# Four transposes of each even attention step move from the middle of the query projection to the gap behind the sums of squares

## The chip, the cores and the metric

The kernel runs on one core of one Trainium2 chip. The metric is the device time of the whole program in microseconds (us), the median of several runs. In the names of the profile PE is TensorE's matrix multiplications, PEld its weight loads, DVE is VectorE, ACT is ScalarE, POOL is GpSimd and SP is the engine that issues most DMAs.

## What is computed

A gated cross-attention layer and then a mixture of experts, on 32 sequences of 64 tokens (2048 rows of 512 numbers), all in float32. The attention has 32 query heads of 128, grouped by four on 8 key-value heads, and normalises each query and key by its root mean square.

```
x = x + tanh(g_xattn[0]) * attention(layernorm(x), ctx)
x = x + tanh(g_ffn[0]) * moe(layernorm(x))
attention:
  q = rmsnorm(h @ Wq.T) ; k = rmsnorm(ctx @ Wk.T) ; v = ctx @ Wv.T
  probs = softmax(q @ k.T / sqrt(128) + mask)
  return (probs @ v) @ Wo.T
moe:
  shared = silu(h @ Gs) * (h @ Us) @ Ds
  top 2 of 16 experts by softmax(h @ gate), weights normalised
  return weighted sum of the experts' outputs + shared
```

## The kernel before, in words

The program has three stages: keys, values and transposed inputs (to 215 us of the profiled run), the attention loop (215 to 1145 us), and the experts with the shared layer (the rest). The change lies in the attention loop alone.

**Number format.** Products that need float32 accuracy are split: an operand x is kept as a rounded high part and the low rest, and `split_product` (lines 549 to 551) adds three products, high by low, low by high and high by high. So ScalarE writes a high part (`pth`, `ah`, `w0h`) and VectorE then subtracts it to get the low part (`ptl`, `al`, `w0l`).

**The loop.** It has 64 steps, numbered i from 0. A step belongs to one pair of sequence blocks and one pair of heads; even and odd steps differ in where their results lie. Each engine has its own hand-written order of the work of a step, and semaphores tie them together. Three steps' work is in flight at a time, so that in step i TensorE issues, in this order (`step`, line 681 on):

- the query projection of step i+1 for head 0 (12 matmuls of 128x512, here "Q") and half of that of head 1 (6 matmuls);
- four transposes (`transpose_probs`, line 642) of the probabilities `pb` that the softmax of step i has made. In an even step they fill the PSUM bank `PS[6]`, in an odd one halves of `PS[2]` and `PS[3]`. They wait for `p_ready`, which VectorE's last two multiplications of the softmax raise (line 1324);
- the other 6 matmuls of the query projection;
- the products of probabilities and values of step i-1 (`probs_v`, line 657), the scores of step i+1 (line 615), and the sums of squares of its queries (`q_sums`, line 623), which the softmax of step i+1 starts from;
- the output products (`outputs`), 12 matmuls into `PS[7]` and 12 into `PS[6]`. The second dozen waits until VectorE has taken the transposes out of `PS[6]` (`pT_evac`).

ScalarE (`act_step`) copies and squares the queries, casts the transposes to `pth` (`probs_hi`, line 1038 in even steps), casts the value products to `ah` (`a_hi_tile`, line 1046; the second pair waits for the first dozen of output products), and takes the exponentials (line 1022). In an even step the cast of line 1038 also waits for the value products of the same step, which still read the `pth` of before.

VectorE (`dve_step`) starts a step with the low part of the transposes (`probs_lo`, line 1333 in even steps) and of the first value products (`a_rest`, line 1290). Then comes `softmax`: it takes the sums of squares out of PSUM (line 1297, `sst`), adds a constant (`qv`, line 1299), and while GpSimd takes the inverse root (line 464) it does what `while_root` holds: it adds the first dozen of output products to the sums `acc` (line 1284) and splits the second pair of value products. Then it scales the scores (line 1306), masks them (1309), takes their maximum (1312) and difference (1315), adds the other dozen of output products, and finishes with sum, reciprocal and two multiplications (1319, 1321, 1324).

The first step (`first=True`) has its transposes behind the sums of squares already and no output products. The last even step, 62 (`last=True` on TensorE), has an order of its own on all three engines. In steps 58 to 61 VectorE has the first parts of the second layer norm to do besides (`residual`, lines 1345 and 1348, 1.4 us a row tile).

Of the kernel before, what the change touches and what calls it, by code (L numbers as in the profile page):

```python
# [63 lines left out]
def build(nc, x, ctxT, wk, wv, w_att, w_shd, mask, g_x, g_f, q_w, k_w, gate, w_gu, w_dn, out):  # L64
# [11 lines left out]
    with ExitStack() as ctx:  # L76
# [129 lines left out]
        with ExitStack() as a:  # L206
# [33 lines left out]
        pT_done, pT_evac, pv_done, a_hi, a_lo, o_done, acc_done = (  # L240
            sem("pT_done"), sem("pT_evac"), sem("pv_done"), sem("a_hi"), sem("a_lo"), sem("o_done"),
            sem("acc_done"))
# [311 lines left out]
        def _(pe):  # L554
# [133 lines left out]
            def step(d, odd, pair_q, w_q, w_before, w_o, q_ready=None, o_ready=None, first=False,  # L688
                     last=False):


                i = 2 * d + odd
                if q_ready is not None:
                    pe.wait_ge(w_lo, q_ready)
                pe.wait_ge(q_sq, 2 * i + 1)
                q_head(0, 1 - odd, pair_q, w_q).then_inc(q_done, 1)
                if last:
                    pe.wait_ge(ss_turned, i + 1)
                    transpose_h2(0, 2)
                    pe.wait_ge(s_scaled, i + 1)  # L700
                    transpose_h2(1, 3)
                pe.wait_ge(q_sq, 2 * i + 2)
                q_head(1, 1 - odd, pair_q, w_q, (0, 1))
                if not first:
                    if not odd:
                        pe.wait_ge(acc_done, 2 * i)
                    transpose_probs(i, odd)
                q_head(1, 1 - odd, pair_q, w_q, (2, 3)).then_inc(q_done, 1)
                if first:
                    pe.wait_ge(s_scaled, 1)  # L710
                    pe.wait_ge(ss_turned, 1)
                else:
                    probs_v(i - 1, 1 - odd)
                if last:
                    pe.wait_ge(h2T_lo, 2)
                scores(d + odd, 1 - odd)
                q_sums(i + 1)
                if last:
                    transpose_h2(2, 0)
                    transpose_h2(3, 1)  # L720
                if first:
                    transpose_probs(i, odd)
                else:
                    outputs(i - 1, w_before, w_o, o_ready)

            pe.wait_ge(w_lo, 4)
# [228 lines left out]
        def _(act):  # L955
# [59 lines left out]
            def squares(h, j):  # L1015
                act.wait_ge(ss_done, j + 1)
                act.activation(sq[:, h].rearrange("p b s -> p (b s)"), PS[h][:], ACT.Square).then_inc(q_sq, 1)
# [22 lines left out]
            def a_hi_tile(i, bp):  # L1040
                if bp == 1:
                    act.wait_ge(o_done, 2 * i + 1)
                    act.wait_ge(a_lo, 4 * i + 6)
                for b2 in range(2):
                    act.wait_ge(pv_done, 2 * i + 3 + b2)
                    act.copy(ah[:, bp, :, b2, :], pv_view(bp, b2)).then_inc(a_hi, 1)  # L1046
# [6 lines left out]
            def act_step(d, odd, w, sl, first=False):  # L1053
                i = 2 * d + odd
                act.wait_ge(s_done, i + 1)
                q_out(0, i + 1)
                squares(0, i + 1)
                if odd:
                    probs_hi(i, 1)
                q_out(1, i + 1)  # L1060
                squares(1, i + 1)
                if not odd:
                    probs_hi(i, 0)
                if not first:
                    a_hi_tile(i - 1, 0)
                    a_hi_tile(i - 1, 1)
                split_slice(i, w, sl)
                exps(i + 1)
# [142 lines left out]
        def _(dve):  # L1211
# [114 lines left out]
            def probs_lo(i, odd):  # L1326
                if odd:
                    for q in range(2):
                        dve.wait_ge(pT_hi, 2 * i + 1 + q)
                        dve.tensor_tensor(pt_odd(1, q), pT_odd(q), pt_odd(0, q), ALU.subtract).then_inc(pT_evac, 1)  # L1330
                else:
                    dve.wait_ge(pT_hi, 2 * i + 2)
                    dve.tensor_tensor(pt_even(1), pT_even(), pt_even(0), ALU.subtract).then_inc(pT_evac, 2)
# [16 lines left out]
            def dve_step(d, odd, w, sl, tile_before, tile, complete=(None, None), first=False):  # L1350

                i = 2 * d + odd
                probs_lo(i, odd)
                if complete[0] is not None:
                    residual(complete[0], 1)
                if not first:
                    a_rest(i - 1, 0)
                if complete[1] is not None:
                    residual(complete[1], 0)

                def while_root():
                    if not first:
                        add_out(2 * i - 1, 1, tile_before)
                        a_rest(i - 1, 1)

                def while_exp():
                    if not first:
                        add_out(2 * i, 0, tile)

                softmax(i + 1, while_root, while_exp)  # L1370
                slice_lo(i, w, sl)
# [370 lines left out]
```

## Time and profile before

| | |
|---|---|
| median of 3 runs | 1465.6 us (1465.59 to 1466.02) |
| the profiled execution, its own time | 1465.77 us |
| its span, first to last instruction | 1464.0 us |
| PE busy | 1419.2 us (97%) |
| PEld busy | 1128.1 us (77%) |
| DVE busy | 847.3 us (58%) |
| ACT busy | 501.0 us (34%) |
| POOL busy | 317.9 us (22%) |
| mean granted clock of TensorE | 0.991 of full speed |

The table reads as follows: the profile is of one execution, so every duration is compared with 1465.77 us, of which 1464.0 us is the span. TensorE is busy nearly always, and the other engines have room on average. "Busy" of PE counts overlapping pipelined matmuls once, so a busy PE can still issue more slowly than it might; the distance from one start to the next shows that.

### The profile page before, as it was taken

To read this page: it belongs to the slowest core of one execution; us is meant where nothing else is said; L and a number is where in the kernel's file an instruction comes from. 1 tells how busy PE (TensorE), PEld (TensorE's weight loads), DVE (VectorE), ACT (ScalarE), POOL (GpSimd) and SP (SyncE) were. 2 spreads that over 40 slices of the span, in tenths; PEclk is the share of its full clock that TensorE was granted. 3 is DMA by queue.
4 is the path that set the end of the run, shared out by engine and by line. 5 is a ranking of instruction groups with operands and counts; after the bars stand their busy time and mean duration, and the time that the engine had idled before them with its cause. 6 is when DMAs were issued, how large, how long until landed. Compare 5 with 4: busy or idle time off the path is not lost.

```text
span 1464.0 us, 27092 instructions
## 1 busy us (share of the span) xinstructions
PE 1419.2 (97%) x9085; PEld 1128.1 (77%) x9086; DVE 847.3 (58%) x1816; ACT 501.0 (34%) x1097; POOL 317.9 (22%) x330
## 2 busy tenths in 40 slices
PE   6999997999999999999999999999999999999995
PEld 5888876787777877778787777877777888777773
DVE  5444446565666656666565666656687653344375
ACT  4333343333333333333333333333334421222220
POOL 1222223212122121211212121121212101232462
PEclk9999999999999999999999999999999999999997
DMA  6544440111111111111101111111122343655565
GB/s 225 164 122 136 122 118 30 47 30 40 37 40 40 30 47 37 34 36 40 41 29 49 37 33 39 38 40 33 59 71 81 126 170 138 230 164 170 153 195 171
DMA packets 91097, 125.95 MB, mean 86 GB/s; under 512 B 7376, under 2 KB 56528, under 8 KB 90512
## 3 DMA queue, kind: packets, MB, share of 16 engines
q1 hardware_dynamic: 84704, 104.16, 22.5%
q0 software_dynamic: 6320, 20.71, 5.1%
q8 instruction: 58, 0.95, 0.3%
q14 instruction: 15, 0.12, 0.0%
HBM read 87.36 MB, written 37.49 MB: 85 GB/s over the span
## 4 chain that ended last, share of the span: by engine, by line
PE 91%; issue 3%; DVE 2%; DMA 2%; POOL 1%; ACT 1%; SPq 0%; POOLq 0%; DVEq 0%; ACTq 0%
PE ps L549 23%; PE ps L551 22%; PE ps L550 22%; PE ps L879 5%; PE ps L615 4%; PE ps L657 4%; PE ps L895 3%; PE ps L623 2%; PE ps L642 2%; PE ps L874 1%; PE ps L596 1%; DMA acc<-in_wv 1%; DMA wgu<-in_w_gu 1%; DVE acc L1660 1%; PE ps L793 1%
## 5 line engine op out<-in xcount | busy, mean ns | idle before, releaser
L1046 ACT CAST ah<-ps 128x256 fp32r<-128x256 f32 x256 | 83.4, 382 | 238.5 <-PE ps L551 234.6
L470 POOL CAST vth<-vt 128x256 fp32r<-128x256 f32 x64 | 25.7, 402 | 637.6 <-PE ps L657 637.6
L1284 DVE TENSOR_TENSOR acc<-ps,acc 128x512 f32 (+1 forms) x129 | 88.6, 687 | 129.9 <-PE ps L551 129.9
L549 PE MATMUL ps<-hT,w0h 128*128 128x512 f32 (+1 forms) x384 | 153.9, 401 | 0.9 <-DVE w0l L1232 0.9
L551 PE MATMUL ps<-hT,w0h 128*128 128x512 f32 (+1 forms) x384 | 150.6, 392 | 0.0
L550 PE MATMUL ps<-hT,w0l 128*128 128x512 f32 (+1 forms) x384 | 150.0, 391 | 0.0
L464 POOL TENSOR_TENSOR qr<-qv,mhalf 128x8 f32<-128x8 f32 x64 | 105.6, 1649 | 90.0 <-DVE qv L1299 90.0
L1290 DVE TENSOR_TENSOR al<-ps,ah 128x256 fp32r<-128x256 f32 x256 | 95.7, 416 | 50.6 <-ACT ah L1046 50.6
L1013 ACT COPY qs<-ps 128x512 f32<-128x512 f32 x128 | 75.2, 587 | 134.9 <-PE ps L551 131.4
L1022 ACT ACTIVATE pb<-pb 128x256 f32<-128x256 f32 x128 | 48.2, 418 | 175.3 <-DVE pb L1315 175.3
L549 PE MATMUL ps<-w1l,ah 128*128 128x512 f32 x260 | 105.3, 405 | 1.0 <-DVE al L1290 1.0
L549 PE MATMUL ps<-w0l,ah 128*128 128x512 f32 x256 | 103.8, 406 | 0.0
L549 PE MATMUL ps<-hT,w1h 128*128 128x512 f32 (+1 forms) x256 | 102.7, 401 | 0.0
L550 PE MATMUL ps<-w1h,al 128*128 128x512 f32 x260 | 102.1, 393 | 0.0
L551 PE MATMUL ps<-w1h,ah 128*128 128x512 f32 x260 | 101.3, 390 | 0.0
L550 PE MATMUL ps<-w0h,al 128*128 128x512 f32 x256 | 100.7, 393 | 0.0
L551 PE MATMUL ps<-hT,w1h 128*128 128x512 f32 (+1 forms) x256 | 100.2, 392 | 0.0
L551 PE MATMUL ps<-w0h,ah 128*128 128x512 f32 x256 | 99.7, 390 | 0.0
L550 PE MATMUL ps<-hT,w1l 128*128 128x512 f32 (+1 forms) x256 | 99.7, 390 | 0.0
L879 PE MATMUL ps<-wgu,xgT 128*128 x376 | 94.8, 382 | 0.3 <-issue 0.2
L551 PEld LDWEIGHTS ps<-hT,w0h 128*128 128x128 f32 x384 | 72.3, 188 | 15.6
L549 PEld LDWEIGHTS ps<-hT,w0h 128*128 128x128 f32 x384 | 72.3, 188 | 15.4 <-DVE w0l L1232 1.1
(223 smaller groups left out, 3033.8 us busy)
## 6 DMA issues: line engine op xcount, KB each, us to landing
wraw<-in_w_att SPq DMA_DIRECT2D x64, 256.0 KB, 2.6
ybuf<-ye SPq DMA_DIRECT2D x47, 256.0 KB, 2.0
vbuf<-vo SPq DMA_DIRECT2D x16, 512.0 KB, 3.3
kbuf<-ko SPq DMA_DIRECT2D x16, 512.0 KB, 3.8
kt<-kbuf SPq DMA_DIRECT2D x32, 256.0 KB, 2.9
vt<-vbuf SPq DMA_DIRECT2D x64, 128.0 KB, 2.0
wgu<-in_w_gu SPq DMA_DIRECT2D x4, 2048.0 KB, 9.3
craw<-in_ctxT SPq DMA_DIRECT2D x9, 512.0 KB, 4.9
```

What stands on the lines that cost most here:

```text
L464: pool.tensor_tensor(qr[:], qv[:], mhalf[:, 0:8], ALU.pow).then_inc(q_rt, 1)
L549: pe.matmul(dst, l_hi, r_lo, start=first, stop=False)
L550: pe.matmul(dst, l_lo, r_hi, start=False, stop=False)
L551: return pe.matmul(dst, l_hi, r_hi, start=False, stop=last)
L615: mm = pe.matmul(PS[3][h * S:(h + 1) * S, b * S:(b + 1) * S], qs[:, h, b], kt[:, b, :], start=True, stop=True)
L657: mm = pe.matmul(PS[4 + b2][:, bp * 256:(bp + 1) * 256], vhl[v_part][rows, bp, :], pt[p_part][rows, 2 * part + bp, :], start=(z == 0), sto ...
L879: mm = pe.matmul(PS[2 + q][:, 0:2 * EI], xgT[q][:, k, :], wgu[:, bass.ds(e, 1), k * 2 * EI:(k + 1) * 2 * EI].rearrange("p a n -> p (a n)") ...
L1013: act.copy(qs[:, h].rearrange("p b s -> p (b s)"), PS[h][:]).then_inc(q_copy, 1)
L1022: act.activation(pb[:, CB * hp:CB * hp + CB, :], pb[:, CB * hp:CB * hp + CB, :], ACT.Exp).then_inc(s_exp, 1)
L1046: act.copy(ah[:, bp, :, b2, :], pv_view(bp, b2)).then_inc(a_hi, 1)
L1284: dve.tensor_tensor(dst, PS[6 + bp][:], dst, ALU.add).then_inc(acc_done, 1)
L1290: dve.tensor_tensor(al[:, bp, :, b2, :], pv_view(bp, b2), ah[:, bp, :, b2, :], ALU.subtract).then_inc(a_lo, 1)
```

## The change

In even steps other than the last, TensorE's four transposes move from between the two halves of head 1's query projection to behind the sums of squares, ahead of the output products, and the query projection runs through its 24 matmuls. Thirty steps (2, 4, ... 60) change so; step 0 has that place already. On ScalarE the cast of the transposes in even steps goes behind the first pair of casts `ah`. On VectorE the low part of the transposes in even steps goes from the head of the step into `while_root`, behind `sst` and `qv` and ahead of the addition of line 1284; this holds for step 0 too. Odd steps keep their order. No instruction is added or taken away, and no semaphore changes its count.

```
# TensorE, step()
-                if not first:
-                    if not odd:
-                        pe.wait_ge(acc_done, 2 * i)
+                if last:
+                    pe.wait_ge(acc_done, 2 * i)
+                if odd or last:
                     transpose_probs(i, odd)
                 q_head(1, 1 - odd, pair_q, w_q, (2, 3)).then_inc(q_done, 1)
...
-                if first:
+                if not odd and not last:
+                    if not first:
+                        pe.wait_ge(acc_done, 2 * i)
                     transpose_probs(i, odd)
-                else:
+                if not first:
                     outputs(i - 1, w_before, w_o, o_ready)
# ScalarE, act_step()
+                if not first:
+                    a_hi_tile(i - 1, 0)
                 if not odd:
                     probs_hi(i, 0)
                 if not first:
-                    a_hi_tile(i - 1, 0)
                     a_hi_tile(i - 1, 1)
# VectorE, dve_step()
-                probs_lo(i, odd)
+                if odd:
+                    probs_lo(i, 1)
...
                 def while_root():
+                    if not odd:
+                        probs_lo(i, 0)
                     if not first:
                         add_out(2 * i - 1, 1, tile_before)
```

On TensorE, in an even step in the loop (`ps<-hT,w0h` and `w0l` are matmuls of the query projection, `ps<-ident,pb` the four transposes), this is the place that they leave:

```order
 L550 MATMUL ps<-hT,w0l 128x512
 L551 MATMUL ps<-hT,w0h 128x512
-L642 MATMUL ps<-ident,pb 128x128 x4
 L549 MATMUL ps<-hT,w0h 128x512
 L550 MATMUL ps<-hT,w0l 128x512
```

The query matmuls now follow one another there. Further on in the same step, on TensorE, between the scores (`ps<-kt,qs`), the sums of squares (`ps<-sq,ones`) and the first output product (`ps<-w0l,ah`):

```order
 L615 MATMUL ps<-kt,qs 64x64 x16
 L623 MATMUL ps<-sq,ones 32x256 x4
+L642 MATMUL ps<-ident,pb 128x128 x4
 L678 REGISTER_ALU
 L549 MATMUL ps<-w0l,ah 128x512
```

The four transposes now stand between the sums and the output products. On VectorE, the head of an even step in the loop before, with the semaphores that each waits for (`ptl<-ps,pth` is the low part of the transposes, `al<-ps,ah` that of value products, `acc<-ps,acc` the addition of output products):

```order
L1333 TENSOR_TENSOR ptl<-ps,pth 128x4x128 [waits pT_hi]
L1289 ISA
L1290 TENSOR_TENSOR al<-ps,ah 128x4x64 [waits a_hi]
L1289 REGISTER_ALU
L1290 TENSOR_TENSOR al<-ps,ah 128x4x64 [waits a_hi]
L1295 REGISTER_ALU
L1297 STREAM_TRANSPOSE sst<-ps 128x256 [waits ss_done]
L1298 REGISTER_ALU
L1299 TENSOR_SCALAR qv<-sst 128x8 [waits ss_turned]
L1281 REGISTER_ALU
L1284 ISA [waits o_done]
L1284 TENSOR_TENSOR acc<-ps,acc 128x512
```

And on VectorE at the same place now (line numbers of the changed kernel are 3 higher there):

```order
L1293 TENSOR_TENSOR al<-ps,ah 128x4x64 [waits a_hi]
L1292 REGISTER_ALU
L1293 TENSOR_TENSOR al<-ps,ah 128x4x64 [waits a_hi]
L1298 REGISTER_ALU
L1300 STREAM_TRANSPOSE sst<-ps 128x256 [waits ss_done]
L1301 REGISTER_ALU
L1302 TENSOR_SCALAR qv<-sst 128x8 [waits ss_turned]
L1335 ISA
L1336 TENSOR_TENSOR ptl<-ps,pth 128x4x128 [waits pT_hi]
L1284 REGISTER_ALU
L1287 ISA [waits o_done]
L1287 TENSOR_TENSOR acc<-ps,acc 128x512
```

The low part of the transposes has moved from the first place to one behind `qv`, directly ahead of the wait for the output products.

## Rows read from the trace of the kernel before

**Rows 1.** The page, part 4: chain that ended last, by engine.

```profile
PE 91%; issue 3%; DVE 2%; DMA 2%; POOL 1%; ACT 1%; SPq 0%; POOLq 0%; DVEq 0%; ACTq 0%
```

**Rows 2.** Waits of PE, 215 to 1150 us: us in total, times, longest.

```profile
PE ps L642 <- DVE pb L1324: 6.7, 3, 4.5
PE ps L615 <- ACT qs L1013: 3.6, 2, 2.9
```

**Rows 3.** Timeline (start, length, idle before), PE, even step: transposes within the query projection.

```profile
595.19 0.39 PE L549 MATMUL ps<-hT,w1h 128*128 x1
...
597.00 0.39 PE L551 MATMUL ps<-hT,w1h 128*128 x1
597.24 0.60 PE L642 MATMUL ps<-ident,pb 128*128 128x128 f32 x4
...
598.37 0.40 PE L549 MATMUL ps<-hT,w1h 128*128 x1
```

**Rows 4.** Timeline, PE, the same step: sums of squares, then output products.

```profile
601.15 0.64 PE L623 MATMUL ps<-sq,ones 128*32 128x256 f32 x8
...
602.53 0.40 PE L549 MATMUL ps<-w1l,ah 128*128 128x512 f32 x1
```

**Rows 5.** Timeline, PE, step 0: sums of squares, transposes, query projection.

```profile
231.21 0.64 PE L623 MATMUL ps<-sq,ones 128*32 128x256 f32 x8
231.78 0.66 PE L642 MATMUL ps<-ident,pb 128*128 128x128 f32 x4
...
232.97 0.40 PE L549 MATMUL ps<-hT,w0h 128*128 128x512 f32 x1
```

**Rows 6.** Timeline, an even step and the odd one behind it: DVE, PEld and PE.

```profile
600.95 0.69 DVE L1333 TENSOR_TENSOR ptl<-ps,pth 128x512 fp32r<-128x512 f32 x1 [3.30 <-ACT pth L1038]
...
604.96 0.69 DVE L1284 TENSOR_TENSOR acc<-ps,acc 128x512 f32 x1 [2.09 <-PE ps L551]
...
610.62 0.76 DVE L1324 TENSOR_TENSOR pb<-pb,rc 128x256 f32<-128x256 f32 x2
...
611.19 0.59 PEld L642 LDWEIGHTS ps<-ident,pb 128*128 128x128 f32 x4
...
615.33 0.64 PE L623 MATMUL ps<-sq,ones 128*32 128x256 f32 x8
...
616.03 0.45 DVE L1297 STREAM_TRANSPOSE sst<-ps 128x256 f32<-128x256 f32 x1 [0.45 <-PE ps L623]
```

**Rows 7.** Timeline, steps 0 and 1: DVE, POOL, and PE's transposes of step 1.

```profile
233.23 0.69 DVE L1333 TENSOR_TENSOR ptl<-ps,pth 128x512 fp32r<-128x512 f32 x1 [2.38 <-ACT pth L1038]
233.84 0.44 DVE L1297 STREAM_TRANSPOSE sst<-ps 128x256 f32<-128x256 f32 x1
...
234.57 1.64 POOL L464 TENSOR_TENSOR qr<-qv,mhalf 128x8 f32<-128x8 f32 x1 [5.20 <-DVE qv L1299]
236.24 0.69 DVE L1306 TENSOR_TENSOR pb<-ps,qr 128x512 f32<-128x512 f32 x1 [1.75 <-POOL qr L464]
...
241.09 0.78 PE L642 MATMUL ps<-ident,pb 128*128 128x128 f32 x4 [4.53 <-DVE pb L1324]
```

**Rows 8.** Scores of step 1; windows: PE, PEld, DVE, ACT, POOL busy, PEclk, DMA.

```profile
245.61 1.15 PE L615 MATMUL ps<-kt,qs 128*64 128x64 f32 x32
...
228.20:231.60 3.40, 1.47 (x40) 1.20 (x40) 2.27 (x6) 2.17 (x5) 1.17 (x1) 1.00 0.00 0
...
241.90:245.20 3.30, 3.30 (x14) 2.28 (x14) 0.83 (x3) 1.49 (x4) 0.00 (x0) 0.50 0.31 79
```

**Rows 9.** Timeline, steps 60 and 61: PE's transposes and scores, DVE's scaling.

```profile
1079.36 0.60 PE L642 MATMUL ps<-ident,pb 128*128 128x128 f32 x4
...
1089.52 0.69 DVE L1306 TENSOR_TENSOR pb<-ps,qr 128x512 f32<-128x512 f32 x1 [0.49 <-POOL qr L464]
...
1094.39 0.77 PE L642 MATMUL ps<-ident,pb 128*128 128x128 f32 x4 [0.70 <-DVE pb L1324]
...
1097.40 0.80 PE L615 MATMUL ps<-kt,qs 128*64 128x64 f32 x20
```

## The prediction

> **What bounds the kernel now.** I read first the chain that ended last: 91% of it is PE [rows 1]. So a saving counts only if it shortens what PE issues, or ends a wait of PE. Next I read who PE waits for in the attention loop: only three waits for the softmax's result, 6.7 us together, and two for query copies [rows 2]. In between the loop is periodic: the transposes of step 26 start at 597.24 and those of step 60 at 1079.36 [rows 3, 9], 482.12 us for 34 steps, 14.18 us each, with no wait of PE at all. So three things can change the time: what the four transposes cost in their two places on PE, the three waits, and a new wait.
>
> **A: the transposes on PE.** In the query projection, the matmul before them starts at 597.00 and the fourth query matmul counted from there at 598.37: 1.37 us for four spacings and the transposes [rows 3]. Undisturbed, neighbours start 0.226 apart (595.19 to 597.00 are eight spacings [rows 3]), four take 0.91. So the transposes cost 1.37 - 0.91 = 0.46 there. Their new place has no row with output products behind it, but step 0 has sums, transposes and 128x512 matmuls in that order: 231.21 to the fourth matmul at 232.97 is 1.76 [rows 5]; without transposes the same stretch is 602.53 - 601.15 = 1.38 [rows 4]. So they cost 0.38 behind the sums: the first weight load after the sums is waited for in either case, and now it is a transpose's. The saving is 0.08 us a step. Thirty steps (2 to 60) change: 30 x 0.08 = **2.4 us**. Bounds: 0 (they cost the same in both places) and 0.46 x 30 = 13.8 (they vanish in the gap of 0.57 that PE has behind the first sum, 231.21 to 231.78 [rows 5]); I take the value from step 0, which is nearly the same sequence.
>
> By the Trainium skill, TensorEngine Tiling (Array Packing), Key Properties, a change of the tiling mode drains TensorE, a change of tile alone does not. The rows agree as far as they go: the sums carry 128*32, what follows them 128*128, and the gap of 0.57 stands there [rows 5]. What follows from it for this change is the second rival.
>
> **B: the wait of step 1.** VectorE's part of the change reaches step 0 too. There `sst` could start at 233.84 only, since the low part of the transposes stood in front of it and waited 2.38 for ScalarE's cast; hence the root at 234.57, the scaling at 236.24 (it waited for the root), and PE's transposes of step 1 at 241.09 after a wait of 4.53 [rows 7]. With `sst` in front: in an undisturbed step it starts 0.70 behind the first sum (615.33, 616.03) [rows 6], so at 231.21 + 0.70 = 231.91 instead of 233.84, 1.93 earlier, and root and scaling with it: the root would end at 234.57 + 1.64 - 1.93 = 234.28. The low part of the transposes, 233.23 to 233.92, then lies under the root, so it costs nothing. From the scaling to the transposes nothing else is waited for. PE's wait falls from 4.53 to 2.6: **1.9 us**.
>
> **C: the clock behind that wait.** From 241.9 to 245.2 the granted clock is 0.50, the 1.2 GHz level, after the engine sat idle for 4.53 us; around it the clock is 1.00, 2.4 GHz [rows 7, 8]. From its transposes to its scores step 1 takes 245.61 - 241.09 = 4.52; step 61, which also starts behind a wait of PE (0.70) but at full clock, takes 1097.40 - 1094.39 = 3.01 [rows 8, 9]. So the slow stretch costs 1.5 us. A wait of 2.6 us lies nearer to the one of 2.9 that ended at 230.13, behind which the clock stayed at 1.00 (228.2 to 231.6) [rows 2, 8], than to 4.53. I take the fall as gone: **1.5 us**; the bounds are 0 and 1.5.
>
> **D: the wait of step 61.** Between the transposes of steps 60 and 61 there are 1094.39 - 1079.36 = 15.03 us instead of 14.18, 0.85 more [rows 9], and the transposes themselves take 0.77 behind the wait against 0.60 without one [rows 3, 9], another 0.17. Cause: in step 60 VectorE has two row tiles of the layer norm besides. Its low part of the transposes waits 3.3 us for ScalarE as in every even step [rows 6], and behind it all is late, so that the scaling at 1089.52 waits for the root [rows 9]. With the low part gone from the head, the first row tile (1.4 us) falls into those 3.3 us; `sst` then comes some 2 us earlier (1.4 and the 0.69 of the low part), the root is no longer last, and the scaling is again tied to the output products as in all other steps. **1.0 us**. The third wait, in step 62, ends on four normalisations that ScalarE does in front of its exponentials; nothing of it moves.
>
> **What is put under cover, and the cover.** VectorE's low part of the transposes (0.69) moves into the time in which VectorE waits for output products, 2.09 us idle ahead of 604.96 [rows 6]. Reckoned from the first sum: transposes from 0.57 on, then ScalarE's cast, the low part from 2.02 to 2.71 (231.21 against 233.23) [rows 5, 7]. The first dozen of output products was done at 604.96 - 601.15 = 3.81 [rows 4, 6], now 0.38 later, 4.19. So 1.5 us are left before the low part would delay line 1284 and all of the softmax behind it. The second dozen on PE also waits for the low part (`PS[6]`): it starts a dozen spacings behind the first, 0.95 + 12 x 0.23 = 3.7, so 1.0 us is left there. ScalarE's `ah` casts come first now, and end before the transposes do, as in an odd step. The addition, 0.38 later against the sums, does not make the odd step's transposes wait: PE too is 0.38 later there. They have little room, though: the softmax ends at 611.38, while their weight loads run from 611.19 to 611.78 and the last two need that end [rows 6]; some 0.1 us. No DMA is moved, and nothing on SP's queue is passed: the loads wait for the same semaphores, and the stages behind the loop hang on PE, so they move up whole.
>
> **The sum.** 2.4 + 1.9 + 1.5 + 1.0 = 6.8 us off the profiled execution's 1465.77 us: 1459.0. The median of the runs is 0.17 below that execution, so 1458.8 us. A measurement of this kernel can tell about 0.2% (2.9 us) from no change.
>
> **Rivals.**
> First, the clock still falls behind the shorter wait of step 1 (C = 0). For it: 2.6 us is more than half of 4.53 and comes only 6 us behind the other wait. Against: the row at 228.2. Time: 1465.6 - 5.3 = 1460.3 us.
> Second, the transposes cost as much behind the sums as they did (A = 0): in both places they stand beside matmuls that are 128*128 like themselves, the gap behind the sums is there with and without them, and the output products may start as slowly behind them as behind the gap. The other terms stay: 1465.6 - 4.4 = 1461.2 us. Step 0's 0.38 speaks against it.
> This second rival is what the Trainium skill's rule (TensorEngine Tiling (Array Packing), Key Properties) would make of the change, since leaving the query projection saves no change of mode.
> Third, slower: the low part of the transposes holds up line 1284 in each even step, because cast or transposes come later than in step 0. It decides from 1.5 us of delay on, plus the 0.1 that the odd step's transposes have; from then on every 0.1 us is paid 30 times, 3 us. To end 0.2% slower it must eat the 6.8 us and 2.9 more, 9.7 / 30 = 0.32 us a step, so a delay of 1.9 us in all: 1468.5 us or more. For it: VectorE runs without a pause from line 1284 to the end of that softmax. Against: 1.5 us of cover, and step 0 shows the cast and low part at their undisturbed times.
> Fourth, B, C and D fail because another semaphore ends last there, and A alone stays: 1463.2 us.
>
> **How the numbers follow.** Forecast, all four terms: 0.58. Clock still falls: 0.19. A = 0: 0.08. A alone: 0.06. Low part in the way, slower: 0.06. More than 2 us better than forecast, with A nearer to its upper bound: 0.03. Faster by over 0.2% (below 1462.7) are the first, second, third and last, 0.88; I leave 0.85, since A = 0 and the slow clock may come together (1462.7). Within 0.2%: 0.08. Slower: 0.07. The range takes in the forecast, the slow clock and A = 0, that is 1458.8 to 1461.2, and 1 us below for A at 0.11 a step: 1457.8 to 1461.5.
>
> **What would show it.** Right: in even steps the distance from one step's sums to the next falls from 28.36 to 28.28 us for a pair of steps; step 1's transposes wait 2.6 us and the clock stays at 1.00 at 242; no wait for VectorE at step 61's transposes; line 1333's successor runs about 2.0 to 2.7 us behind the first sum, with some 1.4 us idle behind it. Wrong: PE waits in odd steps for line 1324's successor, or ahead of the second dozen of output products for the low part.

## The result, and the profile after

The changed kernel takes 1459.43 us (median of 5 runs, 1457.47 to 1459.87). The kernel before takes 1466.02 us beside it (5 runs, 1465.59 to 1466.97). The ratio is 0.995, with an interval of 0.9936 to 0.9965: 6.6 us faster, where 6.8 were forecast. The profiled execution took 1458.22 us, 7.55 less than that of before.

The page of the changed kernel, busy time by engine and the chain that ended last by engine ([rows 1] of before):

```profile
PE 1414.2 (97%) x9085; PEld 1127.7 (77%) x9086; DVE 852.9 (59%) x1816; ACT 502.9 (35%) x1097; POOL 316.4 (22%) x330
...
PE 89%; DVE 3%; DMA 2%; issue 2%; POOL 1%; another core or an unknown queue 1%; ACT 1%; SPq 0%; DVEq 0%; POOLq 0%; ACTq 0%
```

TensorE is as busy as it was (97%), and is still what the chain consists of. So the gain is in what TensorE issues and in its waits. The waits of PE in the loop for these two engines, us in total, times, longest ([rows 2] of before):

```profile
PE ps L615 <- ACT qs L1015: 3.6, 2, 2.9
PE ps L642 <- DVE pb L1327: 2.7, 2, 1.4
```

Line 1327 is line 1324 of before: three waits for the softmax, 6.7 us together, have become two with 2.7, those of steps 1 and 62. The one that is gone is that of step 61; here are the starts of PE's transposes of steps 60 and 61, now in different places of their steps, with no wait named behind either ([rows 9] of before):

```profile
1077.11 0.66 PE L642 MATMUL ps<-ident,pb 128*128 128x128 f32 x4
...
1087.16 0.60 PE L642 MATMUL ps<-ident,pb 128*128 128x128 f32 x4
```

Next the even step, PE of the changed kernel ([rows 3, 4] of before). The first row is the query matmul that stands 15 matmuls ahead of the value products (L657), the last one the first query matmul of the step behind:

```profile
590.86 0.39 PE L549 MATMUL ps<-hT,w1h 128*128 x1
...
594.35 0.38 PE L657 MATMUL ps<-ptl,vth 64*128 64x256 f32 x2
...
596.34 0.64 PE L623 MATMUL ps<-sq,ones 128*32 128x256 f32 x8
596.90 0.66 PE L642 MATMUL ps<-ident,pb 128*128 128x128 f32 x4
597.32 0.48 PE L549 MATMUL ps<-w1l,ah 128*128 128x512 f32 x1
597.63 0.39 PE L550 MATMUL ps<-w1h,al 128*128 128x512 f32 x1
...
598.09 0.40 PE L549 MATMUL ps<-w1l,ah 128*128 128x512 f32 x1
...
602.87 0.39 PE L549 MATMUL ps<-hT,w1h 128*128 x1
```

And rows of before from the same stretches: the first two query matmuls behind the transposes, the first value product, the first two output products and the first query matmul of the step behind. The rows ahead of them are in [rows 3, 4]:

```profile
597.59 0.48 PE L549 MATMUL ps<-hT,w1h 128*128 x1
597.90 0.40 PE L550 MATMUL ps<-hT,w1l 128*128 x1
...
599.16 0.39 PE L657 MATMUL ps<-ptl,vth 64*128 64x256 f32 x2
...
601.72 0.50 PE L549 MATMUL ps<-w1l,ah 128*128 128x512 f32 x1
602.06 0.40 PE L550 MATMUL ps<-w1h,al 128*128 128x512 f32 x1
...
607.33 0.39 PE L549 MATMUL ps<-hT,w1h 128*128 x1
```

The query part took 599.16 - 595.19 = 3.97 us with the transposes in it and takes 594.35 - 590.86 = 3.49 without: 0.48 saved. From the first sum to the next query matmul there were 607.33 - 601.15 = 6.18 us and now there are 602.87 - 596.34 = 6.53: 0.35 paid, 0.13 gained in this step.

The rows beside the transposes show what the 0.13 is made of. The transposes themselves are not cheaper in the new place. In the query projection they put 597.59 - 597.00 = 0.59 us between two matmuls that otherwise start 0.23 apart: 0.36 more. Behind the sums the first output product starts 597.32 - 596.34 = 0.98 us behind the first sum, where it was 601.72 - 601.15 = 0.57: 0.41 more. What differs is the restart, the first few matmuls behind an interruption. In the query projection the first two behind the transposes start 0.31 apart (597.59, 597.90), the next few a little wider than 0.23, and this makes the other 0.12 of the 0.48. Behind the sums the output products start slowly without transposes too (601.72, 602.06: 0.34), and no more slowly with them (597.32, 597.63: 0.31). From the first output product to the next query matmul it took 607.33 - 601.72 = 5.61 us and takes 602.87 - 597.32 = 5.55. So the old place had two slow restarts in a step, and the new one has one. Why the starts are wider there is not shown.

Over the loop the gain is read from the sums of two steps that lie 54 steps, 27 pairs, apart. PE of the changed kernel, steps 3 and 57:

```profile
271.83 0.64 PE L623 MATMUL ps<-sq,ones 128*32 128x256 f32 x8
...
1034.61 0.64 PE L623 MATMUL ps<-sq,ones 128*32 128x256 f32 x8
```

The same two rows of before:

```profile
275.01 0.64 PE L623 MATMUL ps<-sq,ones 128*32 128x256 f32 x8
...
1040.73 0.64 PE L623 MATMUL ps<-sq,ones 128*32 128x256 f32 x8
```

765.72 / 27 = 28.360 us a pair before, 762.78 / 27 = 28.251 after: 0.109 less. The mean is below the 0.13 of the step above because the pairs are not all alike. Before, each of the 27 takes 28.36 us. In the changed kernel 25 take 28.23, and two, behind steps 23 and 39, take 28.47: in each of these the scores of one step last 1.39 us where 1.15 is usual. Those of step 24:

```profile
566.78 1.39 PE L615 MATMUL ps<-kt,qs 128*64 128x64 f32 x32
```

What holds them up is not shown. after_again and step0_old have slow pairs at the same two places, and two_steps, with TensorE's order of before, has one behind step 23.

VectorE in the even step, changed kernel, start, length, idle before ([rows 6] of before):

```profile
597.04 0.45 DVE L1300 STREAM_TRANSPOSE sst<-ps 128x256 f32<-128x256 f32 x1 [0.44 <-PE ps L623]
...
598.42 0.69 DVE L1336 TENSOR_TENSOR ptl<-ps,pth 128x512 fp32r<-128x512 f32 x1 [0.72 <-ACT pth L1040]
600.50 0.69 DVE L1287 TENSOR_TENSOR acc<-ps,acc 128x512 f32 x1 [1.39 <-PE ps L551]
...
606.16 0.76 DVE L1327 TENSOR_TENSOR pb<-pb,rc 128x256 f32<-128x256 f32 x2
```

The low part of the transposes (line 1336) starts 598.42 - 596.34 = 2.08 us behind the first sum and has 1.39 us of idle time behind it: the addition still waits for the output products, not for the low part.

Last the start of the loop: the wait of step 1, its scores, and a window with PE, PEld, DVE, ACT, POOL busy, PEclk, DMA share ([rows 7, 8] of before):

```profile
239.56 0.78 PE L642 MATMUL ps<-ident,pb 128*128 128x128 f32 x4 [1.31 <-DVE pb L1327]
...
242.55 1.15 PE L615 MATMUL ps<-kt,qs 128*64 128x64 f32 x32
...
231.60:235.00 3.40, 3.40 (x17) 2.51 (x10) 1.61 (x4) 1.10 (x2) 1.64 (x1) 0.50 0.31 77
```

The wait is 1.31 us, shorter than forecast, and the scores follow 2.99 us behind the transposes, as at full clock. But the 1.2 GHz level has not gone: it now stands from 231.6 to 235.0, ahead of the wait and not behind it.

The 7.5 us of the two spans then fall into these stretches, each from one start of PE to another: first sum of step 0 to scores of step 1, 14.40 before and 11.22 after (3.18 saved); from there to step 3, 29.40 and 29.28 (0.12); steps 3 to 57, 2.94; steps 57 to 61, 57.75 and 56.47 (1.28); ahead of step 0 and behind step 62 together, 0.0.

### The profile page after: what moved, and what is told of

Read it like the earlier page. It is cut to its first block, busy times and chain, and to the rows that moved or that the text cites. A ratio compares the mean times of both kernels' runs of the same rounds, so it can differ in the third digit from the quotient of the medians.

```text
span 1456.5 us, 27097 instructions
## 1 busy us (share of the span) xinstructions
PE 1414.2 (97%) x9085; PEld 1127.7 (77%) x9086; DVE 852.9 (59%) x1816; ACT 502.9 (35%) x1097; POOL 316.4 (22%) x330
## 4 chain that ended last, share of the span: by engine, by line
PE 89%; DVE 3%; DMA 2%; issue 2%; POOL 1%; another core or an unknown queue 1%; ACT 1%; SPq 0%; DVEq 0%; POOLq 0%; ACTq 0%
PE ps L549 22%; PE ps L550 21%; PE ps L551 21%; PE ps L881 5%; PE ps L615 5%; PE ps L657 4%; PE ps L897 3%; PE ps L623 2%; PE ps L642 2%; PE ps L876 1%; DVE acc L1666 1%; PE ps L596 1%; DMA acc<-in_wv 1%; DMA wgu<-in_w_gu 1%
```

## The experiments

The table gives all kernels that the sections below speak of: the median of the runs (one run where there is no range), the time for a pair of steps between steps 3 and 57, the stretch from the first sum of step 0 to the scores of step 1, and the stretch from step 57 to step 61, all from starts of PE rows as above. The last three are of the profiled execution. The kernel before took 1466.65 us beside dve_act_only, pe_act_only, step0_old and two_steps, 1467.14 beside before_values, behind2, behind4 and ahead2, and 1467.98 beside the last two measurements; the ratios of the sections are to these. Against the 1466.02 of the first comparison they lie 0.6 to 2.0 us higher, so a time in us that was expected is judged with that in mind.

| kernel | time, us | pair | steps 0 to 1 | steps 57 to 61 |
|---|---|---|---|---|
| before | 1466.02 | 28.360 | 14.40 | 57.75 |
| after | 1459.43 (1457.47 to 1459.87) | 28.251 | 11.22 | 56.47 |
| after_again | 1460.00 (1458.28 to 1461.64) | 28.255 | 12.27 | 56.47 |
| dve_act_only | 1463.61 (1460.76 to 1465.58) | 28.360 | 12.49 | 56.72 |
| pe_act_only | 1473.00 (1471.95 to 1475.61) | 28.407 | 15.00 | 60.81 |
| step0_old | 1462.39 (1460.68 to 1467.85) | 28.257 | 15.02 | 56.47 |
| two_steps | 1463.21 (1462.25 to 1465.42) | 28.371 | 11.28 | 56.91 |
| before_values | 1461.09 (1460.61 to 1465.04) | 28.336 | 11.32 | 56.65 |
| behind2 | 1463.49 | 28.233 | 13.77 | 56.47 |
| behind4 | 1486.11 | 28.971 | 14.87 | 58.25 |
| ahead2 | 1476.38 | 28.654 | 13.76 | 58.01 |
| two_waits_less | 1457.80 (1455.48 to 1459.07) | 28.253 | 12.43 | 56.47 |

### The vector and scalar half alone: dve_act_only

TensorE has its old order, VectorE and ScalarE have the new one.

```
# against the changed kernel: TensorE, step()
-                if last:
-                    pe.wait_ge(acc_done, 2 * i)
-                if odd or last:
+                if not first:
+                    if not odd:
+                        pe.wait_ge(acc_done, 2 * i)
                     transpose_probs(i, odd)
...
-                if not odd and not last:
-                    if not first:
-                        pe.wait_ge(acc_done, 2 * i)
+                if first:
                     transpose_probs(i, odd)
-                if not first:
+                else:
                     outputs(i - 1, w_before, w_o, o_ready)
```

> ScalarE's and VectorE's part of the change alone; TensorE keeps its old order, with the transposes of even steps inside the query projection. Theory (the gain is 3.3 us from TensorE's order, A, and the rest from the ends of the waits of steps 1 and 61, B to D): B, C and D stay, so 3 to 4.4 us faster than before, 1461.2 to 1462.7 us, TensorE's step pair stays 28.36 us, the wait of step 61 is gone and that of step 1 is 2.6 us or less. Rival (all gain comes from TensorE's order, the other engines only follow): no gain, 1465 to 1467 us.

1463.61 us, ratio 0.9972 to before (0.9959 to 0.9985). That is 3.0 us below the kernel before beside it, at the lower end of the 3 to 4.4 expected, and 0.9 above the range in us. PE's sums of steps 3 and 57, and the wait for the softmax that is left (two waits, 4.1 us, the longest 2.7):

```profile
274.14 0.64 PE L623 MATMUL ps<-sq,ones 128*32 128x256 f32 x8
...
1039.86 0.64 PE L623 MATMUL ps<-sq,ones 128*32 128x256 f32 x8
...
PE ps L642 <- DVE pb L1325: 4.1, 2, 2.7
```

765.72 us for the 27 pairs, just as before. So A comes with the order on TensorE, and the order on VectorE and ScalarE makes B (step 1's wait 2.7 in place of 4.53) and D (57.75 - 56.72 = 1.03 us) without it. C was not gained here: the clock fell at 240.2.

### The TensorE half alone: pe_act_only

TensorE and ScalarE have the new order; on VectorE the low part stays at the head of the step.

```
# against the changed kernel: VectorE, dve_step()
-                if odd:
-                    probs_lo(i, 1)
+                probs_lo(i, odd)
...
                 def while_root():
-                    if not odd:
-                        probs_lo(i, 0)
                     if not first:
```

> TensorE's and ScalarE's part alone; VectorE keeps the low part of the transposes at the head of the even step. Theory: the head now waits for the transposes behind the sums, so the first value products, the square sums and the root come late: the low part ends 2.7 us behind the first sum, the root 5.7, and the scaling needs the root 0.3 us later than the output products would let it; 0.1 of that is covered, so odd steps wait 0.1 to 0.2 us on TensorE, 30 times, which eats A (3.3 us); step 61 waits 2 us or more and step 1 its 4.5 us as before. Time 1466 to 1471 us. Rival (VectorE's place for the low part does not matter, it has room): A alone, 1462 to 1463 us.

1473.0 us, ratio 1.004 (1.0028 to 1.0052): slower than before, and 2 us above the range expected. VectorE in an even step; its first sum starts at 604.02. Then PEld's waits for the softmax in the loop:

```profile
606.11 0.69 DVE L1336 TENSOR_TENSOR ptl<-ps,pth 128x512 fp32r<-128x512 f32 x1 [5.10 <-ACT pth L1040]
...
614.17 0.76 DVE L1327 TENSOR_TENSOR pb<-pb,rc 128x256 f32<-128x256 f32 x2
...
PEld ps L642 <- DVE pb L1327: 15.1, 31, 4.1
```

Everything on VectorE stands behind a wait of 5.10 us for the cast of the later transposes. The softmax's last multiplication starts 614.17 - 604.02 = 10.15 us behind the first sum; in the changed kernel it is 606.16 - 596.34 = 9.82. Those 0.33 us cost 28.407 - 28.251 = 0.16 a pair, so the odd step has some 0.17 us of room. TensorE's order without VectorE's loses all of A. By the table and its neighbour stretches the loop is 5.0 us longer than before (0.6 at its start, 1.3 over the 27 pairs, 3.1 from step 57 to 61, where the layer norm comes on top). The median is 6.4 above the 1466.65 us that the kernel before took beside it; of the other 1.4 us the profiles say only where such time can lie: the two profiled executions, 7.7 us apart, differ by 2.0 ahead of step 0 and by 0.6 behind step 62, where the edit changes nothing.

### Step 0 as it was: step0_old

```
# against the changed kernel: VectorE, dve_step()
-                if odd:
-                    probs_lo(i, 1)
+                if odd or first:
+                    probs_lo(i, odd)
...
-                    if not odd:
+                    if not odd and not first:
                         probs_lo(i, 0)
```

> The changed kernel with VectorE's old order in step 0 alone. Theory: A and D stay (3.3 and 1.0 us), B and C go: step 1 waits 4.5 us again and the clock falls behind it, 1461 to 1462 us. Rival (B and C were worth nothing, since the slow stretch of the clock falls somewhere anyway): 1459.4 us, as the changed kernel.

1462.39 us, ratio 0.9958 (0.9942 to 0.9974), 2.4 to 3.0 above the two measurements of the changed kernel and 0.4 above the range expected; the intervals of the ratios overlap, so the trace has to tell. All else is as in the changed kernel (pair 28.257, steps 57 to 61 56.47), and steps 0 to 1 take 15.02 us. VectorE's low part in step 0, and PE in step 1:

```profile
235.05 0.69 DVE L1336 TENSOR_TENSOR ptl<-ps,pth 128x512 fp32r<-128x512 f32 x1 [3.26 <-ACT pth L1040]
...
242.90 1.12 PE L642 MATMUL ps<-ident,pb 128*128 128x128 f32 x4 [3.83 <-DVE pb L1327]
...
247.16 1.15 PE L615 MATMUL ps<-kt,qs 128*64 128x64 f32 x32
```

The long wait is back. It is 3.83 and not 4.53 since the clock fell ahead of it too, at 232.2 (TensorE then does the same work more slowly, and the wait is what remains), and a second time at 242.5. The early fall does more here than eat into the wait. From the first sum of step 0 to the transposes of step 1 it takes 15.02 - 4.26 = 10.76 us, in the kernel before 14.40 - 4.52 = 9.88: 0.88 more. The low part waits 3.26 us for the cast of transposes that now run slowly, where it waited 2.38 [rows 7], and the whole softmax stands behind it. So the stretch shows the loss of B, 1.8, and an early fall that costs 0.9 in this order of VectorE. The profiled execution was the longest of its five: 4.8 us of that lie behind step 62, where the edit changes nothing.

### Only steps 0 and 60 on VectorE: two_steps

```
# against the kernel before: VectorE, dve_step()
-                probs_lo(i, odd)
+                late = isinstance(d, int) and i in (0, STEPS - 4)
+                if not late:
+                    probs_lo(i, odd)
...
                 def while_root():
+                    if late:
+                        probs_lo(i, 0)
                     if not first:
```

> The kernel before with VectorE's new order in steps 0 and 60 alone, nothing else moved. Theory: B, C and D without A: 3 to 4.4 us faster than before, 1461.2 to 1462.7 us, with TensorE's step pair at 28.36 us. Rival (in step 60 the low part must go everywhere, or the waits come back in a later step): 1463 us or more.

1463.21 us, ratio 0.9973 (0.9959 to 0.9988): 3.4 us below the kernel before beside it, inside the 3 to 4.4 expected, though 0.5 above the range in us. The pair is 28.371, 0.01 above before through one slow pair; steps 0 to 1 take 11.28 and steps 57 to 61 56.91. So B needs the new order in two steps of VectorE only, and so does D but for 0.2 (57.75 - 56.91 = 0.84 of 1.03): no wait for the softmax is left at step 61, but in step 60 the second dozen of output products starts 0.33 us behind the matmul before it instead of 0.23, and its next spacing is 0.31. A is the rest. Here too the clock fell early, at 233.2, with TensorE's order of before, so the place of the fall does not come from moving the transposes. PE's transposes of step 1:

```profile
241.18 0.77 PE L642 MATMUL ps<-ident,pb 128*128 128x128 f32 x4 [1.38 <-DVE pb L1324]
```

### Another gap for the transposes: before_values

The transposes of the even steps stand at the end of the query projection, ahead of the value products, where the tile changes from 128*128 to 64*128.

```
# against the changed kernel: TensorE, step()
                 q_head(1, 1 - odd, pair_q, w_q, (2, 3)).then_inc(q_done, 1)
+                if not odd and not last and not first:
+                    pe.wait_ge(acc_done, 2 * i)
+                    transpose_probs(i, odd)
...
-                if not odd and not last:
-                    if not first:
-                        pe.wait_ge(acc_done, 2 * i)
+                if first:
                     transpose_probs(i, odd)
-                if not first:
+                else:
                     outputs(i - 1, w_before, w_o, o_ready)
```

> The changed kernel with the four transposes of even steps at the end of the query projection, ahead of the value products, in place of behind the sums; ScalarE and VectorE as changed. Three theories of the 0.11 us a step that the new place saves. (1) It saves what the cut of the query projection costs: here there is no cut either, so even steps take 14.05 us as in the changed kernel, 1459 to 1460 us. (2) It saves since the first weight load behind a change of tiling is waited for anyway, and a transpose's is the one now: here the first load lies under the last query matmul as it did before, so even steps take 14.10 to 14.18 us, 1461 to 1463 us. (3) By the rule that only a change of tiling drains the engine, all places beside 128*128 work cost the same: 14.18 us, 1463 us.

1461.09 us, ratio 0.9967 (0.9956 to 0.9978). A pair takes 28.336: only 0.024 less than in the old place (26 of the 27 take 28.33, 0.03 less). PE there, the last query matmul, the transposes and the first value product:

```profile
595.86 0.39 PE L551 MATMUL ps<-hT,w1h 128*128 x1
596.09 0.60 PE L642 MATMUL ps<-ident,pb 128*128 128x128 f32 x4
596.62 0.39 PE L657 MATMUL ps<-ptl,vth 64*128 64x256 f32 x2
```

From the last query matmul to the first value product there are 596.62 - 595.86 = 0.76 us; in the changed kernel there are 0.32, from 594.03 to 594.35. So the transposes cost 0.44 ahead of a change of tile, 0.48 in the middle of the query projection and 0.35 behind the sums. A change of tile as such is not what makes them cheap. Pair and time lie where theory (2) put them, which shows that the place counts, not that a weight load is the reason. Theory (1) is half right: here too the query projection restarts no second time, but the transposes cost more at this place than the 0.36 they take between query matmuls, and almost nothing is gained.

### How much cover there is: behind2, behind4, ahead2

In the first two, VectorE does two or four more reductions of 128x512 behind the low part in every even step; in the third, two ahead of it. They write a tile that nothing reads.

```
# behind2 (two of them), behind4 (four): VectorE, probs_lo(), even steps
                     dve.tensor_tensor(pt_even(1), pT_even(), pt_even(0), ALU.subtract).then_inc(pT_evac, 2)
+                    dve.tensor_reduce(scr[:, 0, :], maskb[:].unsqueeze(1).to_broadcast([P, 8, S]), AX, ALU.max)
...
# ahead2: the same place
                     dve.wait_ge(pT_hi, 2 * i + 2)
+                    dve.tensor_reduce(scr[:, 0, :], PS[6][:].rearrange('p (b s) -> p b s', s=S), AX, ALU.max)
+                    dve.tensor_reduce(scr[:, 1, :], PS[6][:].rearrange('p (b s) -> p b s', s=S), AX, ALU.max)
                     dve.tensor_tensor(pt_even(1), pT_even(), pt_even(0), ALU.subtract).then_inc(pT_evac, 2)
```

> The changed kernel with two more VectorE instructions of 0.7 us directly behind the low part of the transposes in each even step (1.4 us; they read the mask and write a tile that nothing reads). Theory: the low part has 1.4 to 1.5 us of cover ahead of the output products, so nothing or next to nothing: 1458 to 1462 us. Rival (the cover is not there, VectorE is the bound of the even step): 1.4 us 31 times, over 1490 us.

28.233 a pair, as 25 of the changed kernel's pairs, so two reductions are free. Its time, one run, is 3.5 to 4.1 above the changed kernel's medians and 1.5 above the range expected; of its profile, 1.5 to 2.6 lie in steps 0 to 1, where the clock fell twice (at 233.1 and 243.3).

> The same with four such instructions (2.8 us). Theory: 1.4 us more than the cover, less 0.1 to 0.2 of room in the odd step, so 1.1 to 1.3 us of waiting on TensorE in each odd step, 31 times: 1493 to 1500 us. If the cover were larger than read, the time stays below 1465 us.

28.971 a pair, 0.72 more than the changed kernel, where 1.1 to 1.3 were expected; the time is 7 us below the range. VectorE in an even step (line numbers one higher), PE's first sum of it, and PE's transposes of the odd step behind it:

```profile
610.00 0.69 DVE L1337 TENSOR_TENSOR ptl<-ps,pth 128x512 fp32r<-128x512 f32 x1 [0.72 <-ACT pth L1041]
610.61 0.68 DVE L1338 TENSOR_REDUCE scr<-maskb 128x8 f32<-128x512 f32 x1
...
612.38 0.68 DVE L1341 TENSOR_REDUCE scr<-maskb 128x8 f32<-128x512 f32 x1
612.98 0.69 DVE L1288 TENSOR_TENSOR acc<-ps,acc 128x512 f32 x1
...
607.92 0.64 PE L624 MATMUL ps<-sq,ones 128*32 128x256 f32 x8
...
619.11 0.77 PE L643 MATMUL ps<-ident,pb 128*128 128x128 f32 x4 [0.41 <-DVE pb L1328]
```

The size that failed here was the price of the reductions. They last 0.68 each, but follow one another 0.59 apart: from 610.61 to 612.98 four take 2.37 us, not 2.8. The addition starts 612.98 - 607.92 = 5.06 us behind the first sum, against 600.50 - 596.34 = 4.16 in the changed kernel: 0.90 later. So 2.37 - 0.90 = 1.47 us were covered, the 1.5 of the prediction. Of the 0.90 a pair loses 0.72, so 0.18 is the room of the odd step, where the prediction put some 0.1; pe_act_only gave 0.17.

> The changed kernel with the two instructions (here reading the transposes' bank) ahead of the low part. Theory: the line of the output products is covered as in the run before, but the second dozen of output products waits for the low part, which then ends 4.1 us behind the first sum instead of 2.7, while TensorE is ready at 3.7: 0.4 us or a little more 31 times, 1471 to 1476 us. Rival (TensorE does not need the low part so early): 1458 to 1462 us.

28.654 a pair, 0.40 more, as expected; the time, one run, is 0.4 above the range. Rows of PE's first sum, of VectorE's low part and of the first output product of the second dozen:

```profile
605.33 0.64 PE L624 MATMUL ps<-sq,ones 128*32 128x256 f32 x8
...
608.54 0.68 DVE L1339 TENSOR_TENSOR ptl<-ps,pth 128x512 fp32r<-128x512 f32 x1
...
609.46 0.47 PE L550 MATMUL ps<-w1l,ah 128*128 128x512 f32 x1 [0.16 <-issue]
```

The low part starts 3.21 us behind the first sum and not 2.08, 1.13 later. The second dozen starts 4.13 behind it; in the changed kernel it is 3.81 (600.15 against 596.34), so it is held up by 0.32, and its first spacing is 0.31 and not 0.23 wide (609.46 to 609.77), which makes the 0.40. Cover was therefore 1.13 - 0.32 = 0.81 us, where the prediction said 1.0. The hit on 0.40 comes from errors that cancel: cover 0.2 too large, a delay counted as two durations, 1.4, that was 1.13, and the restart left out.

### The changed kernel again: after_again

Nothing is edited; the question is how far the place of the clock's fall moves the time.

> The changed kernel once more. Theory: the times fall into two groups, by where the one stretch of half clock in the first steps lies: about 1457.5 to 1458.2 us where it lies under a wait (as in the profile of the changed kernel, where it began at 231.6 and shortened the wait of step 1 to 1.3 us), and 1459.4 to 1460 us where it lies in full on work. Rival: one group, the spread is noise.

1460.0 us (1461.64, 1461.49, 1460.0, 1458.28, 1459.18), ratio 0.9948 (0.9934 to 0.9961). The times do not form two separate groups. The profiled one, the 1461.64, shows the clock falling late: PE's transposes and scores of step 1, and two windows (columns as above):

```profile
240.88 1.12 PE L642 MATMUL ps<-ident,pb 128*128 128x128 f32 x4 [2.71 <-DVE pb L1327]
...
245.11 1.15 PE L615 MATMUL ps<-kt,qs 128*64 128x64 f32 x32
...
238.40:241.80 3.40, 0.92 (x5) 0.88 (x6) 2.81 (x7) 1.73 (x4) 0.00 (x0) 0.79 0.00 0
...
241.90:245.20 3.30, 3.30 (x21) 2.42 (x22) 0.76 (x2) 1.54 (x4) 0.00 (x0) 0.71 0.29 79
```

The same kernel, the same order of work, and the fall comes 8.8 us later than in the execution of the first section (at 240.4 in place of 231.6). The wait is 2.71, as forecast, and from transposes to scores it takes 4.23 us in place of 2.99: 1.24 lost. Steps 0 to 1 are 1.05 longer than with the early fall. So the early fall costs about 1.24 - 1.05 = 0.2 us in this order of VectorE, where it does little more than eat into the wait. The two executions are 1461.64 - 1458.22 = 3.4 us apart in all; of the rest, 1.5 lie ahead of step 0 and 0.8 behind step 62, outside what was changed.

### Two waits more: two_waits_less

On top of the change, ScalarE does the exponentials of step 62 ahead of the four normalisations in step 61, and `exps(0)` comes behind the copy and squares of head 0 in step 0.

```
# ScalarE, against the changed kernel
-            for n in range(4):
-                normalise(n)
             exps(i + 1)
+            for n in range(4):
+                normalise(n)
...
             split_first(range(4, 8))
-            exps(0)
...
                 squares(0, i + 1)
+                if first:
+                    exps(0)
```

> The changed kernel with two more edits on ScalarE: in step 0 it copies and squares the queries of head 0 ahead of the first exponentials, in step 61 it takes the exponentials ahead of four normalisations. Theory: the wait for the query copies in step 0 (2.9 us) falls by about 1.1, and the wait of step 62's transposes (1.4 us, 1.8 for the loads) goes, less 0.3 to 0.5 us that transposes of normalised rows now wait: 1.5 to 2.5 us faster than the changed kernel, 1457 to 1458 us at the median. Rival: the waits come back one step on, 1459.4 us.

1457.8 us (1455.48 to 1459.07), ratio to before 0.9934 (0.992 to 0.9947), against 1460.0 for the changed kernel beside it. The intervals of the two ratios overlap; the trace shows the gain in its two places. The waits of PE that are left:

```profile
PE ps L642 <- DVE pb L1328: 2.7, 1, 2.7
...
PE ps L615 <- ACT qs L1015: 1.9, 1, 1.9
```

The wait of step 62 (1.44) is gone, and the distance from step 61 to 62 falls from 17.07 to 15.63; the wait of step 0 for its queries falls from 2.9 to 1.9. That is 2.4 us, and 2.2 is the difference of the medians.

## Why the prediction came out as it did

**The bound** was right: TensorE issues without a pause in the loop, and only what it issues and its few waits counted.

**A, 2.4 us forecast, 3.3 measured (0.109 a step, 30 steps).** The two prices were nearly right, the reason was not. The prediction took the transposes to be cheaper behind the sums since the first weight load there is waited for in either case. The gap behind the first sum is indeed 0.56 to 0.57 us with and without them, but the transposes themselves then cost 0.41 us, more than the 0.36 in the query projection. What is saved is one of two slow restarts of 128x512 matmuls, 0.12 us, and the other one is 0.06 shorter: 0.12 + 0.06 - 0.05 = 0.13. The four spacings that the prediction measured in each place took in most of the restart, which is why 0.46 and 0.38 came near the 0.48 and 0.35 of the whole stretches. Two slow pairs bring the mean from 0.13 down to 0.109. before_values shows that another gap doesn't do. The upper bound (all hidden) was far off: three quarters of the price are paid. The second rival, A = 0, is ruled out by the pair's 28.251 against 28.360. It saw that the output products start slowly behind the transposes as behind the gap, and overlooked that the query projection then no longer starts slowly in its middle. By the rule that stood beside it (the Trainium skill, TensorEngine Tiling (Array Packing), Key Properties) a change of the tiling mode drains the engine; the gap of 0.56 us behind the first sum agrees, with and without transposes. Yet a step became 0.13 us shorter though no change of mode was saved.

**B, 1.9 us forecast, 1.8 measured.** Step 1's wait went from 4.53 to 2.71 in after_again and to 2.7 in dve_act_only, where the clock fell late as in the kernel before. In the profile of the first section it reads 1.31, because the slow stretch lay ahead of it and took the difference.

**C, 1.5 us forecast, 1.3 measured in one profile of the changed kernel and 0.3 in the other.** This step failed in its reason. I took the clock's fall as a consequence of the 4.53 us wait, which a shorter one would spare. It falls in every profile here: early, about the first sum of step 0 (after, two_steps, before_values), late, about the transposes of step 1 (before, after_again, dve_act_only, ahead2, two_waits_less), or at both places (pe_act_only, step0_old, behind2, behind4). Shortly before it there is always a pause of TensorE, the one ahead of step 0's scores (2.9 us, in two_waits_less 1.9) or the wait of step 1, but the 2.9 us pause also stands in executions where no fall follows it, so what decides the place stays open. Where no late fall came, an early one had shortened the wait of step 1 to 1.3 or 1.4 us; a wait of 2.7 us, near the forecast, never went without a fall. That the clock stays at 1.00 behind the 2.9 us wait [rows 8] was true of that execution only: in the changed kernel the fall begins at 231.6, where the row ends. A late fall costs 1.24 in after_again and 1.4 in dve_act_only, an early one about 0.2 in the changed order, against 1.5 in the kernel before. So the first rival was right that a shorter wait doesn't do away with the fall, while the time came out by luck of the place.

**D, 1.0 us forecast, 1.03 measured** by dve_act_only (57.75 to 56.72); the further 0.25 in the changed kernel is A over two pairs.

**The cover** held, and what the third rival needed the experiments had to add by force. The 1.5 us ahead of the addition were 1.47 (behind4), the 1.0 ahead of the second dozen 0.8 (ahead2), the odd step's 0.1 some 0.18. pe_act_only shows the price of leaving out VectorE's half: 0.16 a pair above the changed kernel and no gain at all.

**The sum.** A 0.9 too small and C 0.2 to 1.2 too large nearly cancel: 3.3 + 1.8 + 0.3 to 1.3 + 1.0 = 6.4 to 7.4 us, against 6.8 forecast, 6.6 measured in the first comparison and 8.0 (1467.98 to 1460.0) in after_again's. The spread between single runs of one changed kernel, 2.4 to 7.2 us, is as large as the terms or larger, so the terms rest on the profiles and not on the medians. Where two executions of the changed kernel could be laid side by side, two thirds of the 3.4 us between them lay outside the loop; what makes that part vary stays open.

## What to carry to other kernels

Price a move on the engine that never waits by the whole stretch to the next matmul that stands undisturbed, in both places, and over many repeats of the loop: four spacings gave 0.08 us where the step gained 0.13 and the mean of 27 pairs 0.109. Move the consumers with the work: TensorE's new order alone made this kernel slower, since all of VectorE's hand-written order then stood behind a later result. And count filler and cover in distances between starts, not in durations.

## What the runs showed that I had not expected

- The place of TensorE's clock fall at the loop's start differs between executions of one kernel (231.6 and 240.4), and its price with it (about 0.2 and 1.24 us). A slow stretch ahead of a wait is nearly free only where the end of the wait does not hang on what it slows: with VectorE's old order in step 0 the early fall cost 0.9.
- Four transposes cost TensorE 0.48 us in a run of 128x512 matmuls, 0.44 ahead of the value products and 0.35 behind the sums. Of the 0.48, 0.12 is the slow restart of the matmuls behind them.
- VectorE's reductions of 128x512 that show 0.68 us each follow one another 0.59 us apart in behind4, where none reads what another writes.
